# Counting edges: DVE in POOL's place behind the count matmuls

## The chip, the cores and the metric

The kernel is one program on one core of a Trainium2 chip. The time is device microseconds of one execution; before the change it is 2657.91 us, the median of three runs (2655.0 to 2660.97).

## The reference, cut to what matters

Two graph layers over 625 nodes and 20625 edges, feature width 512. The change touches two pieces of it. The first is the mean over a node's neighbours in layer 0:

```
agg = segment_sum(x[src], dst, 625);  deg = segment_sum(1, dst, 625)
mean = agg / max(deg, 1)
h = mean @ W_l + b + x @ W_r;  h = h * sigmoid(h)
```

The kernel computes it as a matrix product with `AT`, the 625 x 625 matrix that counts the edges from each source to each destination. The second is the radial filter of layer 1, `h = softplus(f_ij @ W1 + b1) - log 2`, `Wij = (h @ W2 + b2) * rcut`, of which the first layer and the softplus are computed beside the counting. Everything else (linear attention, a routed softmax attention, the message passing of layer 1, 128 anchors with a 512 x 512 value matrix each) comes after it.

## The kernel before, in words

Each engine has its own list of instructions, written out by hand, and semaphores order the lists. The edges are cut into `NCH` = 11 chunks of 15 x 125. For every chunk DVE builds one-hot rows (lines 1117 to 1122): `hotS` (125 x 626, the source) and `hotD` (125 x 314, the destination modulo 313, times 1 or 4096). TensorE multiplies the two (line 1720): for each of five slices `s` of 125 sources, 15 matmuls add into one PSUM bank. The destination's lower and upper half share a number: lower count + 4096 x upper count. Both `hotS` and `hotD` have two buffers, so the one-hots of chunk c + 1 wait until PE has ended chunk c - 1 (semaphore `counted`).

After two chunks (after chunks 1, 3, 5, 7, 9 and 10: `COUNTS` = 6) the five banks' sums are unpacked and added up. For slice n: ACT (lines 828 to 840) adds the constant `ROUND` to the sum, which rounds it to a multiple of 4096, and takes `ROUND` off again, into one of two `fields` buffers; DVE (lines 1141 to 1148) subtracts that from the sum in PSUM; POOL (lines 660 to 671) copies both halves into `AT` (first count) or adds them. ACT waits for POOL's `added` before it uses a buffer again. PE takes a bank again when `unpacked` says so.

Beside it runs the softplus of the filters, in 7 pairs of steps: behind chunk c (1 to 7) PE multiplies the pair c - 1 by `W1` (line 1710), ACT computes |z|, relu(z), exp and ln (function `softplus`, lines 804 to 826), and POOL adds relu and ln (line 677). Softplus j + 1 waits for the sums of pair j. After the last pair POOL rounds weight 0 and subtracts (`split_weight(0)`, lines 639 to 645).

After the counting DVE fills two rows of ones and zeros (lines 1150 to 1152, `f_padded`), scales the upper half of `AT` by 1/4096 (line 1154), and the second filter layer begins: ACT `hTh` (line 849), POOL `hTl` (line 685), PE three products, DVE `filt` (line 1164), DMA to HBM.

Of the kernel before, what the change touches and what calls it, by code (L numbers as in the profile page):

```python
# [15 lines left out]
P = 125  # L16
# [12 lines left out]
HALF = 313  # L29
FIELD = 4096.0  # L30
ROUND = 1.5 * 2.0 ** 35
GROUPS = 3
GT = 56
FT = 4
# [96 lines left out]
def count_end(m):  # L131

    return min(COUNT_CHUNKS * (m + 1), NCH) - 1
# [16 lines left out]
def build(nc, A, out):  # L150
    with ExitStack() as ctx:
        def sb(name, shape, dt, scope=ctx):
            return scope.enter_context(nc.sbuf_tensor(name, shape, dt))

        def sem(name):
            return ctx.enter_context(nc.semaphore(name))
# [6 lines left out]
        with ExitStack() as s:  # L163
            radial = sb("radial", [GROUPS * R, 2, FT * P], F32, s)
            cut = sb("cut", [P, GROUPS * GT], F32, s)
            scalarY = sb("scalarY", [P, GROUPS * GT], F32, s)
            factor = sb("factor", [P, GROUPS * GT, 4], F32, s)
            b1c = sb("b1c", [GROUPS * F, 1], F32, s)
            W1d = sb("W1d", [GROUPS * R, GROUPS * F], F32, s)
            W2d = sb("W2d", [GROUPS * F + 1, GROUPS * 128], F32, s)  # L170
            W2h = sb("W2h", [GROUPS * F + 1, GROUPS * 128], F32R, s)
            W2l = sb("W2l", [GROUPS * F + 1, GROUPS * 128], F32R, s)
            soft = sb("soft", [GROUPS * F, 2, FT * P], F32, s)

        with ExitStack() as s:
            RAW = sb("RAW", [128, 2, 2, K, D], F32, s)
# [43 lines left out]
        with ExitStack() as area:  # L220
            with ExitStack() as s:
                hotS = sb("hotS", [P, 2, CH, N + 1], BF16, s)
                hotD = sb("hotD", [P, 2, CH, HALF + 1], BF16, s)
                srcI = sb("srcI", [P, ET], I32, s)
                dstF = sb("dstF", [P, ET], F32, s)
                dstHigh = sb("dstHigh", [P, ET], F32, s)
                dstMod = sb("dstMod", [P, ET], F32, s)
                dstWeight = sb("dstWeight", [P, ET], F32, s)
                with ExitStack() as early:
                    iotaI = sb("iotaI", [P, NT], I32, early)  # L230
                fields = sb("fields", [P, 2, 2, HALF], F32, s)
                AT = sb("AT", [P, T, 2, HALF], F32, s)
                hidden_h = sb("hidden_h", [GROUPS * F, FSTEPS, FT * P], F32, s)
            ATh = sb("ATh", [P, T, NT], F32R, area)
            ATl = sb("ATl", [P, T, NT], F32R, area)
            with ExitStack() as s:
                hTh = sb("hTh", [GROUPS * F + 1, 2, FT * P], F32R, s)
                hTl = sb("hTl", [GROUPS * F + 1, 2, FT * P], F32R, s)
                filt = sb("filt", [P, 2, FT, GROUPS * 128], F32, s)
            with ExitStack() as s:  # L240
                VAh = sb("VAh", [P, T, PAIRS, VW], F32R, s)
                VAl = sb("VAl", [P, T, PAIRS, VW], F32R, s)
            with ExitStack() as s:
                XWh = sb("XWh", [P, T, D], F32R, s)
                XWl = sb("XWl", [P, T, D], F32R, s)
                sb("above_XW", [P, 2 * T * PAIRS * (VW - 2 * DH)], F32, s)
                QTh = sb("QTh", [128, K, NT], F32R, s)
                QTl = sb("QTl", [128, K, NT], F32R, s)
                sig = sb("sig", [P, T, D], F32, s)
                full = sb("full", [128, 3, 1024], F32, s)  # L250
                KVh = sb("KVh", [128, PAIRS, VW], F32R, s)
                KVl = sb("KVl", [128, PAIRS, VW], F32R, s)
# [100 lines left out]
        ids_ready = sem("ids_ready")  # L353
        hot_ready = sem("hot_ready")
        counted = sem("counted")
        unpacked = sem("unpacked")
        added = sem("added")
        at_upper = sem("at_upper")
        at_ready = sem("at_ready")
        at_final = sem("at_final")  # L360
        high_rounded = sem("high_rounded")
        high_ready = sem("high_ready")
        sig_ready = sem("sig_ready")
        x_bias = sem("x_bias")
        silu_step = sem("silu_step")
# [126 lines left out]
        def by_pair(tile_rows):  # L492

            return tile_rows.rearrange("p t (r n) -> p t r n", r=PAIRS)

        def before(n, limit):

# [126 lines left out]
        def _(pool):  # L624
# [4 lines left out]
            g.memset(epsc[:], EPS)  # L629
            g.memset(halfc[:], 0.5)  # L630
            g.memset(roundc[:, 0:1], ROUND)
            g.memset(roundc[:, 1:2], -ROUND)
            g.iota(iotaI[:], pattern=[[1, NT]], base=0, channel_multiplier=0).then_inc(consts_zeroed, 1)
            pool.wait_ge(consts_zeroed, 2)
            g.affine_select(out=ident[:], in_=ident[:], compare_op=ALU.not_equal, fill=1.0, base=0,
# [2 lines left out]

            def split_weight(w):

                if w in (0, WEIGHT["out_W"]):
                    pool.wait_ge(w_loaded[w % 2], 16 * (w // 2 + 1))
                    g.tensor_copy(Wh[w % 2][:], Wraw[w % 2][:]).then_inc(w_rounded, 1)
                pool.wait_ge(w_rounded, w + 1)
                g.tensor_tensor(Wl[w % 2][:], Wraw[w % 2][:], Wh[w % 2][:].bitcast(F32), ALU.subtract).then_inc(w_split, 1)  # L645
# [11 lines left out]
            pool.wait_ge(f_inputs, 2)  # L657
            g.tensor_tensor(W2l[:], W2d[:], W2h[:].bitcast(F32), ALU.subtract).then_inc(f_inputs, 1)

            for c in range(NCH):  # L660
                m = c // COUNT_CHUNKS
                if c == count_end(m):
                    for s in range(T):
                        n = T * m + s
                        pool.wait_ge(unpacked, n + 1)
                        f = fields[:, n % 2]
                        if m == 0:
                            g.tensor_copy(AT[:, s], f).then_inc(added, 1)
                        else:
                            pool.wait_ge(added, n - 4)  # L670
                            g.tensor_tensor(AT[:, s], AT[:, s], f, ALU.add).then_inc(added, 1)
                j = pair_behind(c)
                if j is not None:
                    for i in range(2):
                        n = 2 * j + i
                        pool.wait_ge(f_ln, n + 1)
                        g.tensor_tensor(hidden_h[:, n], hidden_h[:, n], soft[:, i], ALU.add).then_inc(f_hidden, 1)
                if j == FPAIRS - 1:
                    split_weight(0)
            pool.wait_ge(f_padded, 1)  # L680
            for n in range(FSTEPS):
                pool.wait_ge(f_upper, n + 1)
# [93 lines left out]
        def _(act):  # L776
# [51 lines left out]
            for c in range(NCH):  # L828
                m = c // COUNT_CHUNKS
                if c == count_end(m):  # L830
                    for s in range(T):
                        n = T * m + s
                        act.wait_ge(counted, T * c + s + 1)
                        if n >= 2:
                            act.wait_ge(added, n - 1)
                            act.wait_ge(high_ready, n)
                        f = fields[:, n % 2, 1, :]
                        a.activation(f, PS[0:P, count_bank(n), 0:HALF], ACT.Identity, bias=roundc[:, 0:1]).then_inc(high_rounded, 1)
                        act.wait_ge(high_rounded, n + 1)
                        a.activation(f, f, ACT.Identity, bias=roundc[:, 1:2]).then_inc(high_ready, 1)  # L840
                if pair_behind(c) is not None:
                    softplus(pair_behind(c))

# [214 lines left out]
        def _(dve):  # L1058
# [74 lines left out]
            for c in range(NCH):  # L1133
                m = c // COUNT_CHUNKS
                if c < NCH - 1:
                    if c > 0:
                        dve.wait_ge(counted, T * c)
                    for u in range(CH):
                        ins = one_hot(c + 1, (c + 1) % 2, u)
                    ins.then_inc(hot_ready, 1)  # L1140
                if c == count_end(m):
                    for s in range(T):
                        n = T * m + s
                        if n >= 2:
                            dve.wait_ge(added, n - 1)
                        f = fields[:, n % 2]
                        dve.wait_ge(high_ready, n + 1)
                        v.tensor_tensor(f[:, 0, :], PS[0:P, count_bank(n), 0:HALF], f[:, 1, :], ALU.subtract).then_inc(unpacked, 1)

            dve.wait_ge(counted, T * NCH)  # L1150
            v.memset(hTh[GROUPS * F:GROUPS * F + 1].bitcast(F32), 1.0)
            v.memset(hTl[GROUPS * F:GROUPS * F + 1].bitcast(F32), 0.0).then_inc(f_padded, 1)
            dve.wait_ge(added, T * COUNTS)
            link(v.tensor_scalar(AT[:, :, 1, :], AT[:, :, 1, :], 1.0 / FIELD, None, ALU.mult))
            v.memset(ATh[:, :, N + 1:NT].bitcast(F32), 0.0).then_inc(at_final, 1)
            dve.wait_ge(f_inputs, 3)
# [476 lines left out]
        def _(pe):  # L1633
# [78 lines left out]
            for c in range(NCH):  # L1712
                m, parity = c // COUNT_CHUNKS, c % 2
                pe.wait_ge(hot_ready, c + 1)
                for s in range(T):
                    n = T * m + s
                    if c == m * COUNT_CHUNKS and n >= COUNT_BANKS:
                        pe.wait_ge(unpacked, n - COUNT_BANKS + 1)
                    for u in range(CH):
                        ins = mm(PS[0:P, count_bank(n), 0:HALF], hotS[:, parity, u, s * P:(s + 1) * P], hotD[:, parity, u, 0:HALF],  # L1720
                                 start=(c == m * COUNT_CHUNKS and u == 0), stop=(c == count_end(m) and u == CH - 1))
# [3 lines left out]
                if pair_behind(c) is not None:  # L1725
                    first_layer(pair_behind(c))

            pe.wait_ge(unpacked, T * COUNTS)
            pe.wait_ge(f_inputs, 3)
            pe.wait_ge(f_padded, 1)  # L1730

# [334 lines left out]
```

## Time and profile before

| | us |
|---|---|
| profiled execution, its own time | 2659.52 |
| its span | 2657.7 |
| PE busy | 2468.6 (93%) |
| DVE busy | 1795.7 (68%) |
| ACT busy | 923.8 (35%) |
| POOL busy | 1714.6 (65%) |
| mean granted TensorE clock | 0.946 of full speed |

The shares are means over very different stages: the last 1600 us are filled by PE, the first 200 are not. The time of a line of POOL is rough. In what follows a row "2.0 0.5 DVE L10 ... x2 [0.3 <-PE ...]" of the timeline means: two instructions of line 10 that start at 2.0 us and are over 0.5 us later, after 0.3 us in which DVE stood and waited for PE. Instructions of one engine overlap a little, since a duration counts the way through the engine too.

### The profile page before, as it was taken

To read this page: it belongs to the slowest core of one execution; us is meant where nothing else is said; L and a number is where in the kernel's file an instruction comes from. 1 tells how busy PE (TensorE), PEld (TensorE's weight loads), DVE (VectorE), ACT (ScalarE), POOL (GpSimd) and SP (SyncE) were. 2 spreads that over 40 slices of the span, in tenths; PEclk is the share of its full clock that TensorE was granted. 3 is DMA by queue.
4 is the path that set the end of the run, shared out by engine and by line. 5 is a ranking of instruction groups with operands and counts; after the bars stand their busy time and mean duration, and the time that the engine had idled before them with its cause. 6 is when DMAs were issued, how large, how long until landed. Compare 5 with 4: busy or idle time off the path is not lost.

```text
span 2657.7 us, 34630 instructions
## 1 busy us (share of the span) xinstructions
PE 2468.6 (93%) x11680; PEld 2063.2 (78%) x11680; DVE 1795.7 (68%) x2605; ACT 923.8 (35%) x1127; POOL 1714.6 (65%) x769
## 2 busy tenths in 40 slices
PE   6978979986889767999999999999999999999999
PEld 6767868875789766777777777777777777777777
DVE  8864333647579657777777777777777777777775
ACT  3631213532279652232322323232223223232321
POOL 1453403217888844777777777777777777777773
PEclk9989968988699887999999999999999999999999
DMA  3015001002243211221221221221222222212211
GB/s 75 16 47 180 16 32 48 1 1 86 55 123 91 66 43 34 94 95 63 95 95 63 95 93 65 95 86 72 95 79 79 95 72 86 95 66 91 95 63 36
DMA packets 49889, 190.90 MB, mean 72 GB/s; under 512 B 13300, under 2 KB 17911, under 8 KB 33444
## 3 DMA queue, kind: packets, MB, share of 16 engines
q1 hardware_dynamic: 35728, 177.90, 19.2%
q0 software_dynamic: 13200, 10.75, 1.9%
q10 hardware_dynamic: 900, 1.44, 0.2%
q8 instruction: 37, 0.61, 0.1%
q14 instruction: 24, 0.20, 0.0%
HBM read 177.54 MB, written 12.35 MB: 71 GB/s over the span
## 4 chain that ended last, share of the span: by engine, by line
PE 78%; POOL 9%; DVE 7%; issue 3%; ACT 2%; DMA 1%; SPq 0%; ACTq 0%; POOLq 0%; DVEq 0%
PE PS L1645 24%; PE PS L1647 24%; PE PS L1646 24%; POOL gatW L728 5%; PE PS L1720 3%; POOL XN L728 2%; POOL gat L728 1%; DVE hotD L1121 1%; DMA filters<-filt 1%; DVE negmax L1334 1%; DVE hotS L1120 1%; PE PS L1855 1%; PE PS L1897 0%; PE PS L1898 0%; DVE PTl L1351 0%
## 5 line engine op out<-in xcount | busy, mean ns | idle before, releaser
L1594 DVE SCALAR_TENSOR_TENSOR XN<-PS,attn,XN 125x512 f32<-125x512 f32 x1083 | 805.9, 749 | 442.3 <-PE PS L1647 433.7
L766 POOL TENSOR_TENSOR OPl<-TS,OPh 128x1024 fp32r<-128x1024 f32 x256 | 677.3, 2646 | 117.3 <-ACT OPh L1030 117.2
L766 POOL TENSOR_TENSOR OPl<-RAW,OPh 128x1024 fp32r<-128x1024 f32 x192 | 554.9, 2890 | 275.6 <-ACT OPh L1030 275.6
L1645 PE MATMUL PS<-OPh,XTh 128*125 128x512 f32 x1280 | 506.9, 396 | 2.0 <-DVE attn L1548 2.0
L1647 PE MATMUL PS<-OPh,XTl 128*125 128x512 f32 x1280 | 505.6, 395 | 0.0
L1646 PE MATMUL PS<-OPl,XTh 128*125 128x512 f32 x1280 | 503.1, 393 | 0.0
L1030 ACT ACTIVATE OPh<-TS 128x1024 fp32r<-128x1024 f32 x256 | 271.8, 1062 | 529.3 <-PE PS L1647 519.3
L1645 PE MATMUL PS<-OPh,Sh 128*125 128x512 f32 x1024 | 405.3, 396 | 4.5 <-DVE XN L1591 4.5
L1030 ACT ACTIVATE OPh<-RAW 128x1024 fp32r<-128x1024 f32 x192 | 203.9, 1062 | 582.0 <-PE PS L1647 582.0
L1647 PE MATMUL PS<-OPh,Sl 128*125 128x512 f32 x1024 | 404.4, 395 | 0.0
L1646 PE MATMUL PS<-OPl,Sh 128*125 128x512 f32 x1024 | 403.1, 394 | 0.0
L1646 PEld LDWEIGHTS PS<-OPl,XTh 128*125 128x125 f32 x1280 | 238.4, 186 | 60.3
L1647 PEld LDWEIGHTS PS<-OPh,XTl 128*125 128x125 f32 x1280 | 237.6, 186 | 61.1
L1645 PEld LDWEIGHTS PS<-OPh,XTh 128*125 128x125 f32 x1280 | 237.2, 185 | 60.0 <-DVE attn L1548 2.2
L1897 PE MATMUL PS<-hotE,msgh 125*128 125x314 f32 x660 | 201.3, 321 | 35.1 <-DVE msgl L1452 32.0
L1645 PEld LDWEIGHTS PS<-OPh,Sh 128*125 128x125 f32 x1024 | 190.2, 186 | 51.9 <-issue 4.9
L1646 PEld LDWEIGHTS PS<-OPl,Sh 128*125 128x125 f32 x1024 | 190.8, 186 | 48.0
L1647 PEld LDWEIGHTS PS<-OPh,Sl 128*125 128x125 f32 x1024 | 190.5, 186 | 48.3
L1898 PE MATMUL PS<-hotE,msgl 125*128 125x314 f32 x660 | 198.8, 316 | 0.0
L645 POOL TENSOR_TENSOR Wl<-Wraw,Wh 128x2048 fp32r<-128x2048 f32 x15 | 68.9, 4593 | 169.7 <-ACT Wh L794 169.5
L1897 PEld LDWEIGHTS PS<-hotE,msgh 125*128 125x128 f32 x660 | 130.3, 197 | 39.0 <-issue 35.5
L728 POOL DMA_INDIRECT gatW<-nodes,dstI x90 | 140.9, 1565 | 29.0 <-issue 26.5
(335 smaller groups left out, 3647.7 us busy)
## 6 DMA issues: line engine op xcount, KB each, us to landing
RAW<-in_values SPq DMA_DIRECT2D x64, 2048.0 KB, 7.5
filters<-filt SPq DMA_DIRECT2D x14, 672.0 KB
fil<-filters SPq DMA_DIRECT2D x11, 840.0 KB
Wraw<-in_ffn SPq DMA_DIRECT2D x4, 1024.0 KB, 5.4
Wraw<-in_L_q SPq DMA_DIRECT2D x2, 1024.0 KB, 7.1
Wraw<-in_L_k SPq DMA_DIRECT2D x2, 1024.0 KB
Wraw<-in_L_v SPq DMA_DIRECT2D x2, 1024.0 KB, 6.9
gatW<-nodes,dstI POOLq DMA_INDIRECT x90
```

The costliest lines, as they stand in the source:

```text
L645: g.tensor_tensor(Wl[w % 2][:], Wraw[w % 2][:], Wh[w % 2][:].bitcast(F32), ALU.subtract).then_inc(w_split, 1)
L728: g.indirect_dma_start(gats[c % RING][:, u, :], None, nodes, bass.IndirectOffsetOnAxis(ap=dstI[:, t:t + 1], axis=0)).then_inc(gathered[c % ...
L766: g.tensor_tensor(OPl[:, j], operand_source(j, parity), OPh[:, j].bitcast(F32), ALU.subtract).then_inc(op_lower, 1)
L1030: a.activation(OPh[:, j], operand_source(j, parity), ACT.Copy).then_inc(op_upper, 1)
L1120: v.tensor_scalar(hotS[:, parity, u, :], iota16[:, 0:N + 1], srcF[:, bass.ds(t, 1)], None, ALU.is_equal)
L1594: v.scalar_tensor_tensor(out=XN[:, t], in0=PS[0:P, bank, :], scalar=w, in1=XN[:, t], op0=ALU.mult, op1=ALU.add).then_inc(v_added, 1)
L1645: mm(dst, lh, rh, start=start, stop=False, skip_group_check=resumed)
L1646: mm(dst, lh, rl, start=False, stop=False, skip_group_check=resumed)
L1647: return mm(dst, ll, rh, start=False, stop=stop, skip_group_check=resumed)
L1720: ins = mm(PS[0:P, count_bank(n), 0:HALF], hotS[:, parity, u, s * P:(s + 1) * P], hotD[:, parity, u, 0:HALF], start=(c == m * COUNT_CHUNKS ...
L1897: mm(dst, msgh[:, q, u, c_], hot, start=(first and u == 0), stop=False)
L1898: ins = mm(dst, msgl[:, q, u, c_], hot, start=False, stop=(last and u == EB - 1))
```

## The change

ACT copies the sums out of PSUM first (with the constant `CENTRE` = 2047 taken off, so that rounding falls right), and then adds `ROUND` from that copy. That frees the PSUM bank after the first of the two (`copied`). DVE does the rest: it takes `ROUND` off, forms the lower part and adds both parts into `AT`. For that there are five buffers instead of two (`fields_a`, `fields_b`; the first count goes to `AT` itself), and ACT waits only for the addition of one count before. The softplus sums move from POOL to DVE, one chunk later in its list. Weight 0 is rounded by ACT after chunk 9's slices; POOL subtracts it once all one-hots are built. At the end DVE gives the lower half of `AT` its constant back.

```diff
+CENTRE = FIELD / 2 - 1
+            fields_b = sb("fields_b", [P, T - 2, 2, HALF], F32, s)
-                fields = sb("fields", [P, 2, 2, HALF], F32, s)
+                fields_a = sb("fields_a", [P, 2, 2, HALF], F32, s)
+        def count_fields(m, s):
+            if m == 0:
+                return AT[:, s]
+            return fields_a[:, s] if s < 2 else fields_b[:, s - 2]
...
 POOL
-                if w in (0, WEIGHT["out_W"]):
+                if w == WEIGHT["out_W"]:
-            for c in range(NCH):
-                m = c // COUNT_CHUNKS
-                if c == count_end(m):
-                    for s in range(T):
-                        n = T * m + s
-                        pool.wait_ge(unpacked, n + 1)
-                        f = fields[:, n % 2]
-                        if m == 0:
-                            g.tensor_copy(AT[:, s], f).then_inc(added, 1)
-                        else:
-                            pool.wait_ge(added, n - 4)
-                            g.tensor_tensor(AT[:, s], AT[:, s], f, ALU.add).then_inc(added, 1)
-                j = pair_behind(c)
-                if j is not None:
-                    for i in range(2):
-                        n = 2 * j + i
-                        pool.wait_ge(f_ln, n + 1)
-                        g.tensor_tensor(hidden_h[:, n], hidden_h[:, n], soft[:, i], ALU.add).then_inc(f_hidden, 1)
-                if j == FPAIRS - 1:
-                    split_weight(0)
+            pool.wait_ge(hot_ready, NCH)
+            split_weight(0)
...
 ACT
-                        if n >= 2:
-                            act.wait_ge(added, n - 1)
-                            act.wait_ge(high_ready, n)
-                        f = fields[:, n % 2, 1, :]
-                        a.activation(f, PS[0:P, count_bank(n), 0:HALF], ACT.Identity, bias=roundc[:, 0:1]).then_inc(high_rounded, 1)
-                        act.wait_ge(high_rounded, n + 1)
-                        a.activation(f, f, ACT.Identity, bias=roundc[:, 1:2]).then_inc(high_ready, 1)
+                        if m >= 2:
+                            act.wait_ge(added, n - T + 1)
+                        f = count_fields(m, s)
+                        a.activation(f[:, 0, :], PS[0:P, count_bank(n), 0:HALF], ACT.Identity, bias=roundc[:, 1:2]).then_inc(copied, 1)
+                        act.wait_ge(copied, n + 1)
+                        a.activation(f[:, 1, :], f[:, 0, :], ACT.Identity, bias=roundc[:, 0:1]).then_inc(raised, 1)
+                if c == NCH - 2:
+                    weight_upper(0)
...
 DVE
-                        if n >= 2:
-                            dve.wait_ge(added, n - 1)
-                        f = fields[:, n % 2]
-                        dve.wait_ge(high_ready, n + 1)
-                        v.tensor_tensor(f[:, 0, :], PS[0:P, count_bank(n), 0:HALF], f[:, 1, :], ALU.subtract).then_inc(unpacked, 1)
+                        f = count_fields(m, s)
+                        dve.wait_ge(raised, n + 1)
+                        if m == 0:
+                            v.tensor_scalar(f[:, 1, :], f[:, 1, :], ROUND, None, ALU.subtract).then_inc(lowered, 1)
+                            dve.wait_ge(lowered, n + 1)
+                            v.tensor_tensor(f[:, 0, :], f[:, 0, :], f[:, 1, :], ALU.subtract).then_inc(added, 1)
+                        else:
+                            v.scalar_tensor_tensor(out=f[:, 0, :], in0=f[:, 1, :], scalar=ROUND, in1=f[:, 0, :],
+                                                   op0=ALU.subtract, op1=ALU.subtract).then_inc(lowered, 1)
+                            dve.wait_ge(added, n - T + 1)
+                            v.scalar_tensor_tensor(out=AT[:, s, 1, :], in0=f[:, 1, :], scalar=ROUND, in1=AT[:, s, 1, :],
+                                                   op0=ALU.subtract, op1=ALU.add)
+                            dve.wait_ge(lowered, n + 1)
+                            v.tensor_tensor(AT[:, s, 0, :], AT[:, s, 0, :], f[:, 0, :], ALU.subtract).then_inc(added, 1)
+                j = pair_behind(c - 1)
+                if j is not None:
+                    for i in range(2):
+                        n = 2 * j + i
+                        dve.wait_ge(f_ln, n + 1)
+                        v.tensor_tensor(hidden_h[:, n], hidden_h[:, n], soft[:, i], ALU.add).then_inc(f_hidden, 1)
...
             dve.wait_ge(added, T * COUNTS)
+            v.tensor_scalar(AT[:, :, 0, :], AT[:, :, 0, :], CENTRE * COUNTS, None, ALU.add)
...
 PE
-                        pe.wait_ge(unpacked, n - COUNT_BANKS + 1)
+                        pe.wait_ge(copied, n - COUNT_BANKS + 1)
-            pe.wait_ge(unpacked, T * COUNTS)
+            pe.wait_ge(copied, T * COUNTS)
```

## Rows read from the trace of the kernel before

**Rows 1.** Chain that ended last, first 350 us: start us, us, what.
```profile
71.77 0.38 POOL AT L671
...
146.53 4.45 DVE hotD L1121
...
153.30 22.10 PE PS L1720 x150
```

**Rows 2.** Groups of instructions from 25.4 to 179.3 us, costliest first.
```profile
L1720 PE MATMUL PS<-hotD,hotS 125*125 125x313 bf16 x825 | 121.0, 310 | 17.9 <-DVE hotD L1121 16.2 <-DVE XTl L1105 1.7
...
L1121 DVE TENSOR_SCALAR hotD<-iota,dstMod,dstWeight 125x314 bf16<-125x314 f16 x150 | 71.9, 480 | 0.0
L1120 DVE TENSOR_SCALAR hotS<-iota,srcF 125x626 bf16<-125x626 f16 x150 | 61.6, 410 | 1.9 <-PE PS L1720 1.9
```

**Rows 3.** Busy time by stretch: us, PE, PEld, DVE, ACT, POOL, PEclk, DMA share, GB/s.
```profile
89.40:102.50 13.10, 13.06 (x75) 12.12 (x75) 11.16 (x32) 6.78 (x12) 4.69 (x4) 0.78 0.01 1
```

**Rows 4.** Timeline of PE, 20 to 200 us.
```profile
25.55 20.46 PE L1720 MATMUL PS<-hotD,hotS 125*125 125x313 bf16 x150 [1.68 <-DVE XTl L1105]
45.94 1.91 PE L1710 MATMUL PS<-radial,W1d 60*96 60x500 f32 x4
47.79 10.34 PE L1720 MATMUL PS<-hotD,hotS 125*125 125x313 bf16 x75
...
60.87 11.98 PE L1720 MATMUL PS<-hotD,hotS 125*125 125x313 bf16 x75 [0.90 <-DVE hotD L1121]
...
89.44 13.13 PE L1720 MATMUL PS<-hotD,hotS 125*125 125x313 bf16 x75 [2.63 <-DVE hotD L1121]
...
153.30 22.09 PE L1720 MATMUL PS<-hotD,hotS 125*125 125x313 bf16 x150 [10.60 <-DVE hotD L1121]
```

**Rows 5.** Timeline of DVE, 4 to 46 us.
```profile
4.45 0.33 DVE L1114 SCALAR_TENSOR_TENSOR dstMod<-dstHigh,dstF 125x165 f32<-125x165 f32 x1
4.70 0.24 DVE L1115 TENSOR_SCALAR dstWeight<-dstHigh 125x165 f32<-125x165 f32 x1
...
35.93 0.39 DVE L1120 TENSOR_SCALAR hotS<-iota,srcF 125x626 bf16<-125x626 f16 x1 [1.95 <-PE PS L1720]
36.23 0.36 DVE L1121 TENSOR_SCALAR hotD<-iota,dstMod,dstWeight 125x314 bf16<-125x314 f16 x1
...
44.41 0.88 DVE L1148 TENSOR_TENSOR fields<-PS,fields 125x313 f32<-125x313 f32 x2
```

**Rows 6.** Timeline of POOL and DVE, around 146 and 299 us.
```profile
146.22 4.66 POOL L645 TENSOR_TENSOR Wl<-Wraw,Wh 128x2048 fp32r<-128x2048 f32 x1
...
293.38 0.81 DVE L1093 TENSOR_TENSOR QTl<-full,QTh 128x628 fp32r<-128x628 f32 x1
...
299.04 4.63 POOL L645 TENSOR_TENSOR Wl<-Wraw,Wh 128x2048 fp32r<-128x2048 f32 x1
...
299.35 4.99 DVE L1093 TENSOR_TENSOR QTl<-full,QTh 128x628 fp32r<-128x628 f32 x1
```

**Rows 7.** Timeline of ACT, 59 to 281 us.
```profile
59.17 0.67 ACT L816 ACTIVATE soft<-PS,b1c 96x500 f32<-96x500 f32 x1 [2.43 <-PE PS L1710]
...
66.52 0.50 ACT L838 ACTIVATE fields<-PS,roundc 125x313 f32<-125x313 f32 x1
...
67.72 0.52 ACT L838 ACTIVATE fields<-PS,roundc 125x313 f32<-125x313 f32 x1
...
278.71 1.92 ACT L794 ACTIVATE Wh<-Wraw 128x2048 fp32r<-128x2048 f32 x1 [0.53 <-PE PS L1647]
```

**Rows 8.** Timeline of DVE and ACT, 174 to 181 us.
```profile
176.63 0.48 DVE L1148 TENSOR_TENSOR fields<-PS,fields 125x313 f32<-125x313 f32 x1 [1.24 <-ACT fields L840]
...
179.36 1.14 DVE L1154 TENSOR_SCALAR AT<-AT 125x1565 f32<-125x1565 f32 x1
...
179.36 1.13 ACT L849 ACTIVATE hTh<-hidden_h 96x500 fp32r<-96x500 f32 x2 [2.83 <-DVE hTl L1152]
```

**Rows 9.** Groups of DVE instructions over the whole span, shapes kept apart.
```profile
L1574 DVE TENSOR_TENSOR TS<-RAW,TS 128x1024 f32<-128x1024 f32 x63 | 119.4, 1896 | 0.0
```

More of the change, by code:

```diff
@@ L355, in build @@
         counted = sem("counted")
-        unpacked = sem("unpacked")
+        copied = sem("copied")
         added = sem("added")
@@ L360, in build @@
         at_final = sem("at_final")
-        high_rounded = sem("high_rounded")
-        high_ready = sem("high_ready")
+        raised = sem("raised")
+        lowered = sem("lowered")
         sig_ready = sem("sig_ready")
@@ L631, in _ @@
             g.memset(roundc[:, 0:1], ROUND)
-            g.memset(roundc[:, 1:2], -ROUND)
+            g.memset(roundc[:, 1:2], -CENTRE)
             g.iota(iotaI[:], pattern=[[1, NT]], base=0, channel_multiplier=0).then_inc(consts_zeroed, 1)
```

## The prediction

> **What bounds the kernel now.** I read the table of engines and the slices first: PE is the busiest engine, but in the first 180 us it has holes. The chain that ended last, cut to the first 350 us, shows where the counting stage (25.55 to 175.4 us) is decided [rows 1]: not only by PE's counting matmuls, but by POOL's additions into `AT` and by one-hot instructions on DVE of over 4 us. The groups of instructions of that stage [rows 2] say what is odd: 150 `hotD` take 480 ns each, 150 `hotS` 410 ns. Undisturbed, a pair is issued every 0.565 us: the 15 pairs from 35.93 to 44.41 us take 8.48 us [rows 5]. The long ones lie exactly over POOL's instructions: a `hotD` of 4.45 us on the chain [rows 1] stands over the POOL subtraction that runs from 146.22 for 4.66 us [rows 6]. An undisturbed `hotD` takes 360 ns [rows 5], so `hotD` alone loses 150 x (480 - 360) ns = 18 us. So POOL at work stops DVE, DVE is late with the one-hots, and PE waits.
>
> PE's own time [rows 4]: a chunk of 75 matmuls takes 10.3 us at the full clock, a pair of first-layer matmuls 1.85 us more (45.94 to 47.79). Two chunks with their pairs: 24.2 us. They take 28.6 now (chunk 3 starts at 60.87, chunk 5 at 89.44), and the two last ones wait until 153.30. Chunk 5, which started after a wait of 2.63 us, took 13.13 us at a granted clock of 0.78 [rows 3], a mix of both levels, 1.2 and 2.4 GHz; a wait costs PE twice.
>
> **The change, part by part.** Every moment below is on the profiled execution's clock.
>
> Removed: POOL's 30 additions and copies for `AT`, its 14 softplus sums and its rounding of weight 0. With them go the stops of DVE, and the waits of ACT for a free `fields` buffer.
>
> Moved to DVE, for each of 30 slices: instead of one operation on 313 columns it has three (two for the first count). The trace has no such operation with both inputs in SBUF at 313 columns. Nearest rows: two 313-column operations from PSUM take 0.88 us together and one 0.48 [rows 8], so they come every 0.40 us [rows 5]. With both inputs in SBUF, a SCALAR_TENSOR_TENSOR of 165 columns takes 0.33 alone and lets the next instruction start after 0.25 (4.45 to 4.70 [rows 5]), and a TENSOR_TENSOR of 628 columns takes 0.81 alone [rows 6]: (0.81 - 0.33) / 463 = 1.04 ns a column. At 313 columns that is 0.25 + 148 x 1.04 ns = 0.40 in a stream, too. I take 0.40, so 1.2 us a slice and 6.0 us a count; bounds 0.33 (the columns alone) and 0.53 (0.48 and a wait of 0.05, each fully ended before the next begins). A softplus sum of 500 columns is 0.59 by the same rows, 1.17 us a pair, on DVE now.
>
> The Trainium skill has a rule against this (Vector Engine (DVE) Microarchitecture Reference, "Points that are easy to get wrong"): a scalar_tensor_tensor with two SBUF sources that are not bf16 runs at half rate. By it the 165-column row would show at least 0.34 us to the next instruction; it shows 0.25, so the trace speaks against it here. What it would make of the time is the second rival.
>
> Now the queues, chunk by chunk. DVE's two-chunk period: 2 x 8.48 + 6.0 + 2 x 1.17 = 25.3 us, against PE's 24.2. DVE is the bound, by one microsecond. ACT per two chunks: softplus 7.35 each (59.17 to 66.52 [rows 7]) and five slices at 1.16 (the first from 66.52, the second from 67.72, mean with the shorter gaps), 20.5 us, below both. The new loop, where softplus j waits for the sums of pair j-1 in DVE's queue behind a count's slices, is 7.35 + 0.6 + 7.35 + 1.1 + 6.0 + 0.6 = 23 us, also below 25.3.
>
> - DVE ends the one-hots of chunk 2 at 44.41 as now. First count, 5 x 0.8 = 4.0: 48.4. One-hots 3: 56.9; sums 0: 58.1. One-hots 4 wait for PE's chunk 2 (58.13): 66.6. Count 1 waits for ACT (softplus 1 ends 66.5, first slice 67.7): 73.7; sums 1: 74.9; one-hots 5: 83.4.
> - PE: chunk 3 at 60.0, 4 at 72.1, 5 at 84.2, 6 at 96.3, no wait.
> - DVE: sums 2 84.6, one-hots 6 93.1, count 2 99.3, sums 3 100.5, one-hots 7 108.9 (PE wants them at 108.4), sums 4 110.1, one-hots 8 118.6, count 3 124.7, sums 5 125.9, one-hots 9 134.4. PE has ended chunk 8 at 131.3 and waits 3.1 us. Sums 6 135.6, one-hots 10 144.1.
> - PE's chunk 9 from 134.4; after waits of 0.90 and 2.63 us chunks took 11.98 and 13.13 instead of 10.34 [rows 4]. I take the lower one: 146.3, chunk 10 until 156.6 (bounds 155.0 and 157.8; now 175.4).
>
> The tail. ACT rounds weight 0 after count 4's slices (1.92 us [rows 7], ACT has nothing else then, so it costs nothing; uncovered 1.9), until about 149.4. Then POOL subtracts, 4.66 us, until 154.1, over DVE's work of counts 4 and 5. An operation with two SBUF inputs is stopped by POOL too: the one at 299.35 took 4.99 us instead of 0.81, and ended right after POOL's subtraction of 299.04 to 303.67 [rows 6]. So DVE stands with about two operations of count 4 left: 154.1 + 0.8 + 6.0 (count 5) = 160.9. Without the collision DVE would follow PE and end at 156.6 + 1.1 (ACT) + 1.2 = 158.9, at the low bound 157.4. The collision costs 2 to 3 us. The page SBUF — State Buffer of the Trainium skill ("SBUF: two separate sides") says the same of a DVE instruction with two SBUF inputs against GpSimd; the row agrees, and without that rule the sum would be 2 us lower.
>
> Behind it nothing changes: from the end of the last unpacking, 177.11, to the first `hTh` on ACT, 179.36, are 2.25 us [rows 8]. So `hTh` starts at 163.2 instead of 179.36: 16.1 us earlier. The added operation on half of `AT` is one more of 1.14 us [rows 8]; it lies beside ACT's, POOL's and PE's start of the second layer, but can hold POOL's first subtraction. Bounds 0 and 1.1, taken 0.6. Of the DMA queues only the filters' stores follow, shifted as a whole; PE's waits for `copied` come true an operation earlier than those for `unpacked`. The three more buffers cost SBUF room and no time. All after it is a chain that starts at `hTh`, so it moves with it.
>
> Sum: 16.1 - 0.6 = 15.5 us. The profiled execution took 2659.5 (span 2657.7), so 2644.0; the median of the three runs is 1.6 lower, 2657.9, so 2642.4 there.
>
> **Rivals.**
> 1. Each DVE operation pays its full latency (0.53). Then 1.6 us a slice, +0.4 x 25 slices on DVE's path, less some 1 us of its present waits: 9 us less gain, 2652. For it: waits for `lowered` inside a slice. Against: the stream of two in [rows 5], which has waits too. Chance 0.07.
> 2. SCALAR_TENSOR_TENSOR at half rate: two of three operations take 0.33 more, 25 x 0.65 = 16 us, all but 1 of it on DVE's path: gain near 0, 2657. Against: the 165-column row. Chance 0.07.
> 3. Slower: every operation with two SBUF inputs takes what 63 of 1024 columns take late in the kernel, 1.90 us [rows 9], 1.85 ns a column. A slice is then 3 x (0.58 + 0.08) = 1.98 us and a pair of sums 2.0: +0.78 x 25 + 0.83 x 7 = 25 us, 2667. The gain turns into a loss from 1.8 us a slice on. For it: that row's size. Against: 0.81 for 628 columns while POOL stood between two instructions, and POOL is at rest in this stage. Chance 0.03.
> 4. The clock is granted otherwise later on, because the shift sets all waits against it anew; the three runs spread over 6 us, so it can take or give a few, rarely the whole 15. Chance 0.06, half of it no change, a sixth slower.
>
> **How the numbers follow.** The forecast holds 0.77: 2642.5, with its own bounds from 2638 (no collision, full clock: 19.7 us) to 2646. The range goes to rival 1's 2652 and 3 us below the low end for the runs' spread: 2635 to 2652. Less than 0.2%, about 5.3 us, can't be told from no change. Faster: 0.77 + 0.07 + 0.02 = 0.86. Same: 0.07 + 0.03. Slower: 0.03 + 0.01.
>
> **What would show it.** `hotD` back at about 360 ns, no POOL work from 25 to 149 us; three operations of a slice within 1.2 us; chunks 3 to 6 without a wait, chunk 9 waiting some 3 us; the counting ends at 155 to 158 us, `hTh` starts near 163; one DVE operation of several us over POOL's `Wl`. I am wrong if a slice takes 1.6 us or more, if softplus waits for DVE's sums so long that DVE waits for ACT in each count, or if the 16 us at `hTh` are not found again at the end.

## The result and the profile after

The changed kernel takes 2635.8 us in the median of four runs (2634.0 to 2638.0); the kernel before took 2657.5 in the same comparison. The ratio is 0.992, with a 95% interval of 0.9908 to 0.9933: 21.7 us or 0.8% faster. A second comparison, with six and eleven runs, gave 2641.8 against 2660.9, ratio 0.9929 (0.9906 to 0.9951). The forecast was 2642.5, 15.5 us faster, range 2635 to 2652.

| us | before | after |
|---|---|---|
| profiled execution, its own time | 2659.5 | 2634.0 |
| its span | 2657.7 | 2632.1 |
| first count matmul | 25.55 | 25.71 |
| first `hTh` (end of the counting's tail) | 179.36 | 164.53 |
| first `gatW` gather | 682.05 | 668.73 |
| first `square` behind the messages | 999.71 | 972.79 |

The forecast stage gave 14.8 us in these two executions, of 25.6 us between their spans. The rest came much later, in instructions that the change doesn't touch: the stretch from the first `gatW` gather to the first `square`, called the message stage below, is 13.6 us shorter, and 2.8 us are lost elsewhere.

The groups of the counting stage after, 25.4 to 162 us (as [rows 2]; busy us, mean ns, then idle time before them):

```profile
L1727 PE MATMUL PS<-hotD,hotS 125*125 125x313 bf16 x825 | 117.7, 304 | 4.7 <-DVE hotD L1112 3.0 <-DVE XTl L1096 1.7
...
L1111 DVE TENSOR_SCALAR hotS<-iota,srcF 125x626 bf16<-125x626 f16 x150 | 56.0, 373 | 3.7 <-PE PS L1727 3.7
L1112 DVE TENSOR_SCALAR hotD<-iota,dstMod,dstWeight 125x314 bf16<-125x314 f16 x150 | 52.9, 353 | 0.0
...
L806 ACT ACTIVATE soft<-PS,b1c 96x500 f32<-96x500 f32 x14 | 9.4, 669 | 18.2 <-DVE hidden_h L1154 13.5 <-PE PS L1717 4.7
```

`hotD` fell from 480 to 353 ns and `hotS` from 410 to 373, 19.0 and 5.6 us for 150 of each. PE waits 3.0 us for one-hots where it waited 16.2. The price stands on ACT, which waits 13.5 us for the sums in DVE's queue. PE never waits for ACT, and DVE does for 2.4 us.

The shorter one-hots are not all that DVE won. In the kernel before, DVE also stood between the slices of a count, until ACT and POOL had passed a slice on (line 1148, 25.4 to 161.7 us, up to the end of the last one-hot; same columns):

```profile
L1148 DVE TENSOR_TENSOR fields<-PS,fields 125x313 f32<-125x313 f32 x21 | 9.7, 479 | 17.1 <-ACT fields L840 8.9 <-POOL AT L671 7.4 <-POOL AT L668 0.8
```

Added up from DVE's timelines, from the start of the first one-hot to the end of the last (us that each kind of instruction took of DVE's time, overlaps taken off):

| us of DVE's time | before | changed | `pool_busy` (below) |
|---|---|---|---|
| one-hots | 108.2 | 85.1 | 109.0 |
| waits inside the counts | 17.1 | 0.9 | 0 |
| operations of the counts | 8.9 | 21.6 | 21.5 |
| softplus sums | 0 | 8.3 | 8.2 |
| waits for PE | 1.9 | 3.7 | 2.0 |
| total | 136.2 | 119.5 | 140.7 |

So 23.1 us of shorter one-hots and 16.2 us of waits paid for 21.0 us of added work. With the waits gone and the one-hots as long as before, DVE loses 4.5 us (`pool_busy`, below); with the shorter one-hots alone it would come out about even, an estimate from the same rows.

The timeline of PE after (answers to [rows 4]):

```profile
25.71 21.99 PE L1727 MATMUL PS<-hotD,hotS 125*125 125x313 bf16 x150 [1.68 <-DVE XTl L1096]
...
61.60 10.33 PE L1727 MATMUL PS<-hotD,hotS 125*125 125x313 bf16 x75
...
85.82 10.33 PE L1727 MATMUL PS<-hotD,hotS 125*125 125x313 bf16 x75
...
110.32 10.33 PE L1727 MATMUL PS<-hotD,hotS 125*125 125x313 bf16 x75 [0.21 <-DVE hotD L1112]
...
135.57 23.34 PE L1727 MATMUL PS<-hotD,hotS 125*125 125x313 bf16 x150 [2.81 <-DVE hotD L1112]
```

From chunk 3 (61.60) to chunk 5 (85.82) are 24.2 us, PE's own time; there were 28.6. The two waits left are those forecast: before chunk 7, and before chunk 9. The timeline of DVE and POOL after shows a slice, and then POOL's subtraction over count 5:

```profile
94.60 0.47 DVE L1142 SCALAR_TENSOR_TENSOR fields_a<-fields_a 125x313 f32<-125x313 f32 x1
95.00 0.47 DVE L1145 SCALAR_TENSOR_TENSOR AT<-fields_a,AT 125x313 f32<-125x313 f32 x1
95.39 0.47 DVE L1148 TENSOR_TENSOR AT<-AT,fields_a 125x313 f32<-125x313 f32 x1
95.78 0.47 DVE L1142 SCALAR_TENSOR_TENSOR fields_a<-fields_a 125x313 f32<-125x313 f32 x1
...
151.89 4.52 POOL L653 TENSOR_TENSOR Wl<-Wraw,Wh 128x2048 fp32r<-128x2048 f32 x1 [126.60 <-ACT Wh L784]
...
152.77 3.99 DVE L1142 SCALAR_TENSOR_TENSOR fields_a<-fields_a 125x313 f32<-125x313 f32 x1 [1.52 <-ACT fields_a L829]
...
161.82 0.47 DVE L1148 TENSOR_TENSOR AT<-AT,fields_b 125x313 f32<-125x313 f32 x1
```

The operations of a slice come every 0.40 us, 1.18 a slice, and the one that meets POOL takes 3.99 instead of 0.47 and ends with it. The tail (as [rows 8]), DVE and ACT:

```profile
164.52 1.14 DVE L1160 TENSOR_SCALAR AT<-AT 125x1565 f32<-125x1565 f32 x1
165.58 1.97 DVE L1161 TENSOR_SCALAR AT<-AT 125x1565 f32<-125x1565 f32 x1
...
164.53 1.13 ACT L840 ACTIVATE hTh<-hidden_h 96x500 fp32r<-96x500 f32 x2 [4.46 <-DVE hTl L1158]
```

### The profile page after: what moved, and what is told of

Its sections match the earlier page's. It is cut to its first block, busy times and chain, and to the rows that moved or that the text cites. A ratio compares the mean times of both kernels' runs of the same rounds, so it can differ in the third digit from the quotient of the medians.

```text
span 2632.1 us, 34596 instructions
## 1 busy us (share of the span) xinstructions
PE 2463.6 (94%) x11680; PEld 2058.3 (78%) x11680; DVE 1807.2 (69%) x2675; ACT 924.3 (35%) x1128; POOL 1645.4 (63%) x724
## 4 chain that ended last, share of the span: by engine, by line
PE 83%; DVE 10%; POOL 2%; ACT 2%; DMA 2%; issue 1%; SPq 0%; DVEq 0%; ACTq 0%; POOLq 0%
PE PS L1652 25%; PE PS L1654 24%; PE PS L1653 24%; PE PS L1904 3%; PE PS L1905 3%; PE PS L1727 2%; DVE hotS L1111 1%; DVE hotD L1112 1%; POOL XN L718 1%; POOL gatW L718 1%; DMA filters<-filt 1%; DVE negmax L1341 1%; PE PS L1862 1%; DVE XN L1075 0%; DVE PTl L1358 0%
## 5 line engine op out<-in xcount | busy, mean ns | idle before, releaser
L718 POOL DMA_INDIRECT gatW<-nodes,dstI x90 | 131.2, 1458 | 30.4 <-issue 26.2
```

Source lines behind the costliest of these rows:

```text
L718: g.indirect_dma_start(gats[c % RING][:, u, :], None, nodes, bass.IndirectOffsetOnAxis(ap=dstI[:, t:t + 1], axis=0)).then_inc(gathered[c % ...
```

## The experiments

Times are medians. The runs were made in three series, each with its own runs of the kernel before: 2661.0 us (first series: `pool_busy` to `before_split`), 2657.0 (second: the three delays and `pads_on_pool`), 2660.9 (third: the rest). The changed kernel itself ran only in the third. Single executions of one kernel scatter by 10 us and more (the kernel before in the second series: 2650.4 to 2663.7), so the small effects are read from the profiled executions, at the first `hTh`, and the median only confirms them.

**Is it POOL's work that stopped DVE?** `pool_busy`: the changed kernel with 30 more additions on POOL, whose results nobody uses. Only POOL's own later work, the subtraction of weight 0 and `hTl`, stands behind them.

```diff
...
+            for n in range(T * COUNTS):
+                pool.wait_ge(copied, n + 1)
+                if n > 0:
+                    pool.wait_ge(spare_step, n)
+                g.tensor_tensor(spare, flat[:, 0:2 * HALF], flat[:, 2 * HALF:4 * HALF], ALU.add).then_inc(spare_step, 1)
...
```

> The changed kernel, with 30 additions of 125x626 on POOL beside it that nobody waits for (each starts when ACT has copied a slice out of PSUM; they read X and write XN, which are free then, so the result stays). Theory A (the gain of the counting stage is that POOL at work no longer stops DVE's instructions): POOL is busy 30 x 1.25 = 38 us, DVE is stopped for a good part of it, its instructions become long by about 1 us each time, and as DVE is the bound the kernel loses 15 to 35 us: 2650 to 2670. Rival B (the gain is the shorter chain ACT - DVE - POOL and the three more buffers): nothing waits for the new work, so 2636, no change.

Measured: 2671.4 us against 2661.0 before in that series, ratio 1.0038 (1.0014 to 1.0061), 1 us above the range of theory A. The whole gain is gone and 10 us more. Its groups from 25.4 to 162 us, when 22 of the 30 additions had started (same columns):

```profile
L1123 DVE TENSOR_SCALAR hotD<-iota,dstMod,dstWeight 125x314 bf16<-125x314 f16 x146 | 70.4, 482 | 0.0
L1122 DVE TENSOR_SCALAR hotS<-iota,srcF 125x626 bf16<-125x626 f16 x146 | 58.8, 403 | 2.0 <-PE PS L1738 2.0
L677 POOL TENSOR_TENSOR XN<-X 125x626 f32<-125x626 f32 x22 | 53.6, 2436 | 83.9 <-ACT fields_a L838 66.6 <-ACT AT L838 15.6
```

`hotD` is back at 482 ns, as before the change. The first `hTh` is at 186.64, 22 us later than in the changed kernel, and the table above says where they were lost: in the one-hots, 24 us, with DVE's other work as in the changed kernel. Rival B as it was put, no change with POOL at work, is out. The test says nothing against the shorter chain as such: DVE's waits inside the counts, 17.1 us before, stay away in `pool_busy` too. The other case, short one-hots with these waits kept, was tried in no run.

POOL's operations suffer as well, but not evenly. Half of the 30 additions take 1.46 us or less, and four take 8.8 to 11.5 us. One of these, in POOL's timeline:

```profile
102.35 8.78 POOL L677 TENSOR_TENSOR XN<-X 125x626 f32<-125x626 f32 x1
```

DVE runs a count and a pair of sums, all operations with two inputs, back to back from 102.80 to 109.98, those of the count in their usual 0.47 us. Here it is POOL that stands, until 1.15 us after DVE's run has ended.

**Do the buffers matter?** `two_buffers`:

```diff
-            return fields_a[:, s] if s < 2 else fields_b[:, s - 2]
+            return fields_a[:, (T * m + s) % 2]
...
-                        if m >= 2:
-                            act.wait_ge(added, n - T + 1)
+                        if n >= T + 2:
+                            act.wait_ge(added, n - 1)
```

> The changed kernel with two buffers in place of five (slice n waits for the addition of slice n - 2). Theory A: ACT takes 1.0 us a slice and DVE 1.19, so two buffers nearly suffice; at most 2 us slower, 2636 to 2638. Rival B (the buffers carry the gain): ACT and DVE wait for each other in each count, 1.5 us x 5 = 7 us slower or more, 2643 and up.

Measured: 2640.7, ratio 0.9913 (0.9884 to 0.9943). Four runs from 2634.5 to 2649.6 can't decide between 2638 and 2643; the profiled execution can. `hTh` is at 164.13, no later than in the changed kernel (164.53, and 163.49 in a second execution), with the same two waits of PE (0.80 and 3.10 us in place of 0.21 and 2.81). The three more buffers bring nothing that these runs can show.

**The softplus sums alone.** `sums_on_pool` takes them out of DVE's list and puts them ahead of `split_weight(0)` in POOL's:

```diff
...
+            for j in range(FPAIRS):
+                for i in range(2):
+                    n = 2 * j + i
+                    pool.wait_ge(f_ln, n + 1)
+                    g.tensor_tensor(hidden_h[:, n], hidden_h[:, n], soft[:, i], ALU.add).then_inc(f_hidden, 1)
```

> The changed kernel with the 14 softplus sums back on POOL, in the place where ln ends. Theory A: a pair of sums on POOL stopped DVE for 1.9 us before the change (a hotD of 1.30 and a hotS of 1.36 in place of 0.36 and 0.39), on DVE it takes 1.17. DVE is the bound, so six pairs cost 6 x 0.8 = 4 to 5 us: 2640. Rival C (the wait of softplus for DVE's queue costs more than it looks): ACT waits 13.5 us less for sums, and the kernel is faster than 2636.

Measured: 2642.2, ratio 0.993 (0.9907 to 0.9953), 1.5 us more than `two_buffers` in the same series, which the scatter hides. `hTh` at 166.66, 2 to 3 us later; PE's waits in its timeline:

```profile
85.39 10.33 PE L1726 MATMUL PS<-hotD,hotS 125*125 125x313 bf16 x75 [1.26 <-DVE hotD L1117]
...
112.12 11.98 PE L1726 MATMUL PS<-hotD,hotS 125*125 125x313 bf16 x75 [2.44 <-DVE hotD L1117]
...
138.94 22.11 PE L1726 MATMUL PS<-hotD,hotS 125*125 125x313 bf16 x150 [2.72 <-DVE hotD L1117]
```

The one-hots take 98.5 us of DVE's time here, 13.4 more than in the changed kernel, where the sums take 8.3 themselves. So 14 sums on idle POOL cost more than on DVE, the bound engine, since they stop DVE longer than it would take itself. Of the 15 us 2 to 3 belong to them. Rival C is out.

**Weight 0 alone.** `before_split` is the kernel before with one edit: ACT rounds weight 0 after chunk 9's slices, and POOL subtracts after the fifth `hTl`.

```diff
...
-                if j == FPAIRS - 1:
-                    split_weight(0)
...
+                if n == 4:
+                    split_weight(0)
...
+                if c == NCH - 2:
+                    weight_upper(0)
```

> The kernel before, with weight 0 alone treated otherwise: ACT rounds it after the slices of chunk 9, POOL subtracts after the fifth hTl. Theory A: the two one-hots of 4.31 and 4.53 us (142 to 151 us) go back to 0.36, 8 us less, PE's chunk 9 starts at 145 instead of 153, and the whole is 8 us faster: 2649. Rival: PE or ACT is late next at that place and takes half of it back, 2653.

Measured: 2650.0 against 2661.0, ratio 0.9958 (0.9944 to 0.9972), 11 us. In its profiled execution `hTh` stands at 174.09, 5.3 us earlier, and chunk 9 at 147.19, not 145. That the median came to the 2649 that was expected is luck: the stage gave 5.3 us, and the rest is not shown to come from the edit. I had booked both long one-hots whole. The first of them, 4.31 us, covered a softplus pair's 2.44 us too, which stays here; the timeline of DVE shows it:

```profile
142.03 1.29 DVE L1123 TENSOR_SCALAR hotD<-iota,dstMod,dstWeight 125x314 bf16<-125x314 f16 x1
143.25 1.35 DVE L1122 TENSOR_SCALAR hotS<-iota,srcF 125x626 bf16<-125x626 f16 x1
```

**Where the other 11 us are.** Three kernels with k = 2, 4 and 8 more memsets, each waited for, in DVE's tail of the counting (k stands for the number):

```diff
+            for _ in range(k):
+                link(v.memset(hTh[GROUPS * F:GROUPS * F + 1].bitcast(F32), 1.0))
```

> The changed kernel with two more one-row memsets ahead of the end of the counting's tail (about 1.0 us each, on the path). The profiled executions of before and after differ by 14.8 us until the gathers of the message stage (745 us), and by 25 us behind them; POOL's gather issues took 1565 ns before and 1458 after. Theory D (chance: the gathers meet DVE's instructions in another phase each time the stretch ahead of them gets longer or shorter): the time is not 2636 + 2.0, but off it by up to several us either way. Rival E (something of the change itself makes the message stage shorter): 2638, and that stage as long as in the changed kernel.

> As the one with two, with four memsets: theory D somewhere in 2636 to 2647, the message stage of another length than in the changed kernel; rival E 2640 and the same length.

> As the one with two, with eight memsets: theory D somewhere in 2639 to 2652; rival E 2644 and the message stage as long as in the changed kernel.

Measured: 2643.2, 2643.3 and 2650.0, against 2657.0 before: 14, 14 and 7 us faster, ratios 0.9944 (0.9923 to 0.9966), 0.9951 (0.9929 to 0.9972) and 0.9969 (0.9953 to 0.9984). All three lie 3 to 6 us above rival E's numbers and inside theory D's wide ranges. But both were counted from 2636, and the changed kernel had no run in this series; from the 2641.8 of the next one, the delays of 2 to 9 us give about what was measured. That speaks against a phase that the delay sets, but single runs of one kernel differ by 17 us (`delay_4`: 2637.7 to 2655.2). So I ran both kernels again.

> The changed kernel once more, for its time and for a second profiled execution. In the first comparison it was 21.7 us faster than before, while the counting stage alone gave 14.8. The executions so far, those of the kernel before too, scatter over 10 us and more. Theory D' (the message stage, from the first gatW gather to the next layer's first square, takes another length in each execution, whatever the kernel): over more executions the gain comes down to the stage's 15 to 16 us, and the message stage of this execution is anywhere from 304 to 319 us, not 304.06 again. Rival E (the change makes that stage shorter): the gain stays at 21 us and the stage near 304.

> The kernel before, one more profiled execution. Theory D': hTh near 179 again, and the message stage of another length than 317.66. Rival E: 317 again.

Measured: 2641.8 against 2660.9 for the changed kernel, 19.1 us faster, and one execution of 2656.1 for the one before. The gain didn't come down to 15 or 16 us, as theory D' had it; with an interval of 13 to 25 us the median can't say. The two ends of the message stage in the second execution of the changed kernel:

```profile
665.98 1.22 POOL L718 DMA_INDIRECT gatW<-nodes,dstI  x1 [1.84 <-PE PS L1654]
```

```profile
979.06 0.63 ACT L1031 ACTIVATE square<-XN 125x512 f32<-125x512 f32 x1 [1.26 <-DVE XN L1075]
```

It is 313.08 us long, in the first one it was 304.06. All profiled executions together, sorted by the number of gather issues that took over 3.5 us (most take 1.2 to 2.3):

| execution | first `hTh` | long issues | message stage, us |
|---|---|---|---|
| changed | 164.53 | 1 | 304.06 |
| `before_split` | 174.09 | 1 | 303.98 |
| `delay_2` | 164.11 | 3 | 309.21 |
| `pads_on_pool` | 156.54 | 3 | 309.65 |
| before, again | 179.42 | 3 | 311.15 |
| `pads_again` | 159.55 | 3 | 312.09 |
| `sums_on_pool` | 166.66 | 4 | 313.25 |
| `delay_4` | 167.99 | 4 | 315.73 |
| before | 179.36 | 4 | 317.66 |
| changed, again | 163.49 | 5 | 313.08 |
| `delay_8` | 171.09 | 5 | 316.06 |
| `pool_busy` | 186.64 | 6 | 318.99 |
| `two_buffers` | 164.13 | 6 | 319.26 |
| `split_later` | 159.03 | 6 | 321.71 |

A long issue, from POOL's timeline of the kernel before and of the changed one:

```profile
887.66 4.65 POOL L728 DMA_INDIRECT gatW<-nodes,dstI  x1 [0.30 <-issue]
892.62 1.21 POOL L728 DMA_INDIRECT gatW<-nodes,dstI  x1 [0.30 <-issue]
```

```profile
891.38 4.65 POOL L718 DMA_INDIRECT XN<-nodes,dstI  x1 [0.31 <-issue]
```

The stage's length follows the number of long issues (1 to 6, some 3 us each, 4.65 in place of 1.21), and that number follows neither the kernel nor the delay: the same code has 1 and 5, and 3 and 4. The 135 issues of the stage add up to 203.4 us in the first execution of the changed kernel and to 213.8 in that of the kernel before, which is 10.4 of the 13.6 us; in all fourteen they add up to 203 to 219 us, and what is left of the stage is 100 to 104. So the profiled pair of executions happened to compare 4 with 1. Rival E has no support: the eleven executions with the change in them average 313.9 us, the three without it 310.9. Theory D as I first put it, a phase set by the shift, isn't supported either; that the length differs from execution to execution (D') is shown.

What a long issue has in common with the others can be read, though no run tried it. Around the first one above, DVE runs eight two-input operations for the messages back to back from 886.93 on. The last of them:

```profile
889.74 1.48 DVE L1452 TENSOR_TENSOR msgl<-msg,msgh 125x1280 fp32r<-125x1280 f32 x1
```

It ends at 891.22, and the issue at 892.31. Each of the 54 long issues of the fourteen executions ends 1.1 to 1.3 us after such an `msgl`: POOL stands until DVE's run is over, as its additions did in `pool_busy`. But other issues start at the same place of the run and take 1.4 us. What decides which of them is held stays open.

**Two edits further.** `split_later` moves POOL's subtraction of weight 0 behind the fifth `hTl`; `pads_on_pool` and `pads_again`, one kernel, also give POOL the two padding rows, which DVE no longer fills:

```diff
...
-            pool.wait_ge(hot_ready, NCH)
-            split_weight(0)
+            pool.wait_ge(f_inputs, 3)
+            pool.wait_ge(counted, T * NCH)
+            g.memset(hTh[GROUPS * F:GROUPS * F + 1].bitcast(F32), 1.0).then_inc(pad_step, 1)
+            pool.wait_ge(pad_step, 1)
+            g.memset(hTl[GROUPS * F:GROUPS * F + 1].bitcast(F32), 0.0).then_inc(f_padded, 1)
...
+                if n == 4:
+                    split_weight(0)
```

> The changed kernel; POOL fills the two padding rows as soon as the last count matmul has ended (159 us), while DVE still adds the last slices, and subtracts weight 0 after the fifth hTl instead of at 152 us. Both take work off the tail: the first hTh can start near 161.3 instead of 164.5, and DVE no longer stands 3.5 us behind POOL. Theory A: 3 to 3.5 us faster, 2632.5. Rival: the subtraction among the hTl makes the second filter layer later by what is won, 2636.

> The kernel with the padding rows on POOL and weight 0 subtracted after the fifth hTl, once more: against the changed kernel in the same call, hTh starts some 5 us earlier at the same count of slow matmul chunks, and the median is 3 to 6 us lower.

> The changed kernel with the subtraction of weight 0 alone moved behind the fifth hTl. DVE then meets no POOL in counts 4 and 5; it follows PE's last count matmul by ACT's two operations and its own three: 2.4 us, in place of 3.4. About 1 us faster at hTh when the last two chunks run at a lower clock, up to 3 when they run at the full one. In the median 1 to 2 us.

Measured: `pads_on_pool` 2636.8 (before 2657.0), 0.9917 (0.9886 to 0.9949), which is the rival's number and not the 2632.5 expected, but both were counted from a changed kernel that had no run beside it; `pads_again` 2636.5 (changed again 2641.8, before 2660.9), ratio to before 0.9899 (0.9876 to 0.9923) against 0.9929 (0.9906 to 0.9951) for the changed kernel; `split_later` 2641.8, 0.9927 (0.9904 to 0.9951). The intervals overlap, but five executions of `pads_again` (2631.5 to 2637.4) lie below all six of the changed kernel (2638.4 to 2649.8). At the tail the gain is plain: with chunks 9 and 10 in 23.42 us in both executions, `hTh` is at 159.55 against 163.49, 3.9 us earlier where some 5 were expected. ACT's first `hTh` then no longer waits for DVE; the timeline of POOL and ACT in `pads_again`:

```profile
157.60 0.93 POOL L671 MEMSET hTh<- 1x1000 f32 x1 [132.31 <-PE PS L1730]
158.59 0.93 POOL L673 MEMSET hTl<- 1x1000 f32 x1
...
159.55 1.13 ACT L846 ACTIVATE hTh<-hidden_h 96x500 fp32r<-96x500 f32 x2 [0.92 <-POOL hTl L673]
```

For `split_later` compare `delay_2`, whose chunks 9 and 10 took 20.46 us too: `hTh` 159.03 against 164.11, less the two memsets of the delay, one every 1.16 us: 161.8. That is 2.8 us, the upper end of what was expected. In the median, 2641.8 for both kernels, it can't be seen.

## Why the prediction came out right, step by step

- **The bound.** POOL stops DVE, DVE is late, PE waits: `hotD` was to go back to 360 ns and went to 353; `pool_busy` brought back 482. But this is only a part of it. The other part, DVE's own waits of 17.1 us inside the counts, has neither a name nor a size in the forecast. It is right in the sum because the new queues were built up from their start, with a DVE that waits for ACT once.
- **A slice.** 1.2 us forecast, 1.18 measured; SCALAR_TENSOR_TENSOR and TENSOR_TENSOR of 313 columns from SBUF are alike (0.47 us, one every 0.40). Rivals 1 to 3, full latency, half rate and the 1.9 us of 1024 columns, are out. The half rate for scalar_tensor_tensor that the Trainium skill gives (Vector Engine (DVE) Microarchitecture Reference, "Points that are easy to get wrong") doesn't hold here: a SCALAR_TENSOR_TENSOR with two f32 inputs from SBUF took 471 ns for 313 columns, as long as the TENSOR_TENSOR beside it.
- **The queues.** Forecast: no wait of PE for chunks 3 to 6, 0.5 us before 7, 3.1 before 9. Measured: none, 0.21, 2.81. ACT stays uncritical, with 13.5 us of waits for sums.
- **PE's clock.** The first two chunks took 21.99 us instead of 20.46, which no step had: 1.5 us. Chunks 9 and 10 took 23.34, forecast 22.2, within the bounds. In other executions of kernels with the change the first pair took 20.46 or 22.1 and the last one 20.46, 22.1 or 23.4. The last one moves `hTh` by up to 3 us: 156.54 and 159.55 in `pads_on_pool` and `pads_again`, one kernel. PE had waited 2.8 us ahead of it in both, so "a wait costs PE twice" is too strong: it did so in some executions and not in others. The profile's windows show the granted clock at 0.87 of full speed in the last pair, a mix of the two levels, after PE had stood 2.81 us:

```profile
135.50:159.00 23.50, 23.34 (x150) 22.32 (x150) 21.92 (x55) 11.44 (x20) 4.52 (x1) 0.87 0.01 1
```

- **The tail.** The collision with POOL: forecast that DVE's operation stands until POOL ends and the tail costs 2 to 3 us. It stood 3.5; DVE ended at 162.3 (forecast 160.9), `hTh` 164.53 (forecast 163.2). As the last matmul ended later, the collision cost 1 us in this execution, 3 where the clock was full (`delay_2` and `split_later`). Nor does DVE always stand: in `delay_2` POOL's subtraction began amid DVE's run, at 147.21, and took 10.02 us. The second operation on `AT` met POOL's first subtraction, 1.97 us instead of 1.14; POOL's pair of `hTl` took 3.06. The first `filt` is 14.8 us earlier than before (169.06 for 183.87), so of the bounds 0 and 1.1 it was nearly 0.
- **The sum.** 15.5 us forecast for the stage, 14.8 measured in one pair of executions, 15.9 in the other (179.42 and 163.49). From the first `hTh` to the first `gatW` gather the two executions take 502.69 and 504.20 us, so the shift is passed on, within 1.5 us, as forecast.
- **What the sum didn't have.** The message stage scatters over 18 us from execution to execution. It was in rival 4 only as a scatter of the clock, from a spread of 6 us over three runs, too few to see it: in the three series the kernel before spreads over 13 to 18 us. The median gain, 21.7 of four runs each and 19.1 of six and eleven, has intervals that hold 15.5 only in the second comparison (13 to 25 us); the rest beyond the stage's 15 to 16 us is not shown to belong to the change. By the stage alone the first median would have come to about 2642, as forecast; the rest took it to 2635.8, 0.8 us above the low end of the range. That it stayed inside is luck, since nothing in the forecast sized this scatter. The whole difference of 25.6 us between the two profiled spans is 13.3 up to the first `gatW` gather (14.8 from the counting, less 1.5 on the way), 13.6 in the message stage, and 1.3 lost behind it.

## What to carry to other kernels

An engine with time to spare isn't free when its work stops another: 19 and 6 us on one-hots vanished when 52 us of POOL's additions went, although the engine that took them over was the bound already. A chain through three engines costs too: the bound engine stood 17 us in its counts, and taking over the last link ended 16 of them. Look for instructions of one shape whose mean lies a third above their minimum, and at what stands over the long ones. And before a gain of the whole is believed, find it in the stage where the edit is; here 14.8 of 25.6 us were.

## What the runs showed that I had not expected

- POOL is slowed too: an addition of 626 columns took 1390 ns in the mean in the kernel before, and 2492 for the 30 of `pool_busy`, because four of them stood over DVE's back-to-back two-input operations, for 8.8 to 11.5 us each.
- Issues of an indirect gather by POOL take 1.21 us at the least and up to 2.4 beside DVE's work, but 1 to 6 of 135 take 4.4 to 4.8, in changing places in each execution, and every one of these ends just after a run of such operations.
